# Windowed attention of a fused gate network: scores and values in 64x64 products over the visible keys only, values in two banks, and another order of steps

## The reference, cut to what matters

```python
WINDOW = 128
bk, bv = look_around(bk), look_around(bv)      # keys of the window before, then of this one: 256
sim = jnp.einsum('bhwid,bhwjd->bhwij', bq, bk) # 128 queries x 256 keys
mask = (i < j) | (i > j + WINDOW) | (j == -1)
sim = jnp.where(mask, -jnp.finfo(sim.dtype).max, sim)
attn = jax.nn.softmax(sim, axis=-1)
out = jnp.einsum('bhwij,bhwjd->bhwid', attn, bv)
```

## Time and profile before

| what | value |
|---|---|
| median of 3 runs | 5209.54 us (5208.2 to 5211.27) |
| the profiled execution | 5208.83 us |
| its span in the trace | 5207.0 us |
| granted TensorE clock over the span | 0.997 |
| PE matmul busy | 5089.8 us, 98% |
| DVE busy | 3371.8 us, 65% |
| ACT busy | 2933.1 us, 56% |
| POOL busy | 2614.3 us, 50% |

### The profile page before, as it was taken

The page is one execution under the profiler, slowest core; times in us unless marked ns, Lnnn a source line. Parts: engine busy times, 40 slices in busy tenths (PEclk is TensorE's granted clock), DMA queues, the critical chain, the costliest instruction groups (busy, mean ns, idle before and its releaser), DMA issues.

```text
span 5207.0 us, 177128 instructions
## 1 busy us (share of the span) xinstructions
PE 5089.8 (98%) x72856; PEld 4142.8 (80%) x72856; DVE 3371.8 (65%) x8313; ACT 2933.1 (56%) x7591; POOL 2614.3 (50%) x2308
## 2 busy tenths in 40 slices
PE   7999999999999999999999999999999999999998
PEld 5887888878888788887888887788777887878787
DVE  6656676666766667666676665766657676566764
ACT  4556555555555565555655556555556555565554
POOL 5445555455544456444464543645436455455543
PEclk9999999999999999999999999999999999999999
DMA  2211111111111211111121111201211112111110
GB/s 82 98 69 54 59 36 66 46 65 48 39 62 47 71 42 39 63 61 56 42 67 36 62 55 46 65 31 62 66 41 60 43 51 67 46 54 59 35 50 17
DMA packets 51392, 280.81 MB, mean 54 GB/s; under 512 B 5280, under 2 KB 22688, under 8 KB 33696
## 3 DMA queue, kind: packets, MB, share of 16 engines
q1 hardware_dynamic: 39840, 252.69, 13.2%
q0 software_dynamic: 10752, 16.78, 1.7%
HBM read 249.01 MB, written 28.84 MB: 53 GB/s over the span
## 4 chain that ended last, share of the span: by engine, by line
PE 96%; issue 1%; DVE 1%; ACT 1%; POOL 1%; SPq 0%; DMA 0%; POOLq 0%; ACTq 0%; DVEq 0%
PE bank_M L729 11%; PE bank_S L712 10%; PE bank_S L714 9%; PE bank_S L713 9%; PE bank_F L660 7%; PE bank_F L661 6%; PE bank_F L662 6%; PE bank_F L916 6%; PE bank_M L748 5%; PE bank_F L806 5%; PE bank_M L837 5%; PE bank_F L849 4%; PE bank_F L821 4%; PE bank_M L756 2%; PE bank_F L788 1%
## 5 line engine op out<-in xcount | busy, mean ns | idle before, releaser
L1497 POOL TENSOR_TENSOR q_lo<-q_mix,q_hi 128x512 fp32r<-128x512 f32 x512 | 668.4, 1306 | 1233.6 <-ACT q_hi L981 1233.6
L994 ACT ACTIVATE probs<-bank_S,neg_max 128x512 f32<-128x512 f32 x1024 | 700.9, 685 | 778.8 <-DVE neg_max L1227 688.7
L1227 DVE TENSOR_REDUCE neg_max<-bank_S 128x1 f32<-128x512 f32 x1024 | 696.2, 683 | 303.3 <-PE bank_S L714 300.0
L712 PE MATMUL bank_S<-k_hi,q_lo 128*128 128x512 f32 x2048 | 876.8, 428 | 7.2 <-POOL q_lo L1497 5.1
L714 PE MATMUL bank_S<-k_hi,q_hi 128*128 128x512 f32 x2048 | 805.7, 393 | 0.0
L713 PE MATMUL bank_S<-k_lo,q_hi 128*128 128x512 f32 x2048 | 805.0, 393 | 0.0
L729 PEld LDWEIGHTS bank_M<-mixer_n,probs 64*64 64x64 f32 x32768 | 528.1, 135 | 188.9 <-issue 165.8
L1492 POOL TENSOR_TENSOR q_mix<-q_rope,w_pre 128x256 f32<-128x256 f32 x1024 | 631.6, 638 | 52.2 <-POOL q_lo L1497 0.9
L1523 POOL TENSOR_TENSOR l_probs<-l_probs,l_inv 128x1024 f32<-128x1024 f32 (+1 forms) x256 | 429.2, 1682 | 396.1 <-DVE l_inv L1330 396.1
L729 PE MATMUL bank_M<-mixer_n,probs 64*64 64x64 f32 x32768 | 600.4, 222 | 14.0 <-issue 9.9
L1053 ACT ACTIVATE l_probs<-l_probs,l_least 128x256 f32<-128x256 f32 (+1 forms) x1024 | 480.5, 472 | 185.2 <-DVE l_least L1310 183.6
(11 more groups left out here) (142 smaller groups left out, 10173.8 us busy)
## 6 DMA issues: line engine op xcount, KB each, us to landing
w_qkv_hi<-split_qkv SPq DMA_DIRECT2D x30, 1536.0 KB, 6.7
w_qkv_lo<-split_qkv SPq DMA_DIRECT2D x30, 1536.0 KB, 6.3
w_hi<-split SPq DMA_DIRECT2D x30, 1408.0 KB, 6.1
w_lo<-split SPq DMA_DIRECT2D x30, 1408.0 KB, 8.3
w<-in_w SPq DMA_DIRECT2D x32, 768.0 KB, 4.2
w_o<-in_w_o SPq DMA_DIRECT2D x32, 512.0 KB, 5.2
x_in<-in_x POOLq DMA_DIRECT2D x16, 512.0 KB, 3.8
out_y<-in_x SPq DMA_DIRECT2D x16, 512.0 KB, 7.7
```

Source lines behind the costliest of these rows:

```text
L712: mm(bank[k][:], q_lo[q], k_hi[:, s, :], start=(s == 0), stop=False)
L994: fn(probs[:, n % PB, :], bank[k][:], ACT.Exp, bias=neg_max[:, n % 2:n % 2 + 1], accum_out=row_sum[:, n % 4:n % 4 + 1]).then_inc(emptied[k ...
L1227: v.tensor_reduce(neg_max[:, n % 2:n % 2 + 1], bank[k][:], AX.X, ALU.max, negate=True)\
L1497: g.tensor_tensor(q_lo[:, c % QB], q_mix[:], q_hi[:, c % QB].bitcast(F32), ALU.subtract)\
```

## The change

Scores: each product takes 64 queries (half a window) and only the keys that these may see, 192 for t > 0; for t = 0 it takes 64 keys for the lower queries and 128 for the upper ones. Head of the pair (row half of the PE array) and query half (column half) make four 64x64 tiles. Values: each product takes 64 keys, 64 features and 64 queries; keys 0-63 of a window go to bank M0, keys 64-127 to M1, and the two wholly masked blocks are left out (24 products instead of 8; 16 instead of 4 for t = 0). ACT copies M0 to `o_locT`, then DVE adds M1 to it in place of its copy. A `local_values` thus needs both M banks, which it holds until both are done.

```diff
+SEEN = P // 2
+BLOCKS_SEEN = [((0, 0, True, False), (0, 0, True, True)), ((0, 1, False, True), (1, 0, True, False)),
+               ((1, 1, True, True), (1, 1, False, True))]
+BLOCKS_AT_START = [((0, 1, True, True),) * 2, ((1, 1, True, True),) * 2]
...
     if kind == "local_values":
-        return [LOCAL]
+        return ["M0", "M1"]
...
                 for pair in range(2):
                     hp = 2 * quad + pair
-                    for parity in range(2):
-                        k = f"F{parity}"
-                        rows = slice(HD * parity, HD * (parity + 1))
-                        last = mm(bank[k][:, pair * 2 * P + lo:(pair + 1) * 2 * P],
-                                  qT[rows, hp, t * P:(t + 1) * P],
-                                  kT[rows, hp, (t - 1) * P + lo:(t + 1) * P], start=True, stop=True)
-                        if pair == 1:
-                            last.then_inc(filled[k], 1)
+                    for half in range(2):
+                        queries = slice(half * SEEN, (half + 1) * SEEN)
+                        first = P if t == 0 else half * SEEN
+                        final = P + (half + 1) * SEEN
+                        for parity in range(2):
+                            rows = slice(HD * parity, HD * (parity + 1))
+                            last = mm(bank[f"F{parity}"][queries, pair * 2 * P + first:pair * 2 * P + final],
+                                      qT[rows, hp, t * P + queries.start:t * P + queries.stop],
+                                      kT[rows, hp, (t - 1) * P + first:(t - 1) * P + final], start=True, stop=True)
+                            if pair and half:
+                                last.then_inc(filled[f"F{parity}"], 1)
...
-                if now.was_filled(step, LOCAL):
-                    pe.wait_ge(emptied[LOCAL], now.fill(step, LOCAL) - 1)
-                lo = 1 if t == 0 else 0
+                for k in banks_of(step):
+                    if now.was_filled(step, k):
+                        pe.wait_ge(emptied[k], now.fill(step, k) - 1)
                 for pair in range(2):
-                    for j in range(lo, 2):
-                        for parity in range(2):
-                            h = 4 * quad + 2 * pair + parity
-                            last = mm(bank[LOCAL][HD * parity:HD * (parity + 1), pair * P:(pair + 1) * P],
-                                      v_loc[:, t - 1 + j, h * HD:(h + 1) * HD], pT[:, pair, 2 * parity + j, :],
-                                      start=(j == lo), stop=(j == 1))
-                last.then_inc(filled[LOCAL], 1)
+                    for one in (BLOCKS_SEEN if t else BLOCKS_AT_START):
+                        for r, (half, j, start, stop) in enumerate(one):
+                            keys = slice(r * SEEN, (r + 1) * SEEN)
+                            for parity in range(2):
+                                h = 4 * quad + 2 * pair + parity
+                                last = mm(bank[f"M{r}"][HD * parity:HD * (parity + 1),
+                                                        pair * P + half * SEEN:pair * P + (half + 1) * SEEN],
+                                          v_loc[keys, t - 1 + j, h * HD:(h + 1) * HD],
+                                          pT[keys, pair, 2 * parity + j, half * SEEN:(half + 1) * SEEN],
+                                          start=start, stop=stop)
+                            if pair and one[0][0]:
+                                last.then_inc(filled[f"M{r}"], 1)
...
+            def local_values(step, l, u):
+                t, quad = u // QUADS, u % QUADS
+                act.wait_ge(filled["M0"], now.fill(step, "M0"))
...
+                fn(o_locT[:, 2 * quad:2 * quad + 2, :], bank["M0"][:, 0:2 * P].rearrange("p (c i) -> p c i", c=2), ACT.Copy)\
+                    .then_inc(emptied["M0"], 1)
...
-                dve.wait_ge(filled[LOCAL], now.fill(step, LOCAL))
...
-                v.tensor_copy(o_locT[:, 2 * quad:2 * quad + 2, :],
-                              bank[LOCAL][:, 0:2 * P].rearrange("p (c i) -> p c i", c=2)).then_inc(emptied[LOCAL], 1)
+                dve.wait_ge(filled["M1"], now.fill(step, "M1"))
+                dve.wait_ge(emptied["M0"], now.fill(step, "M0"))
+                to = o_locT[:, 2 * quad:2 * quad + 2, :]
+                v.tensor_tensor(to, bank["M1"][:, 0:2 * P].rearrange("p (c i) -> p c i", c=2), to, ALU.add)\
+                    .then_inc(emptied["M1"], 1)
```

All three order texts are replaced. Of `ORDER` two lines before and after show the kind of edit:

```diff
-up.1.1 scores.63 mixers.31 mix.30 norm up.1.2 up.1.3 mix.31 scale up.1.4 values.7 x_turn.0 talk_v up.1.5 talk_k talk_q
-down.1.0 down.1.1 down.1.2 down.1.3 project.3
+up.1.3 up.1.4 up.1.5 mix.30 x_turn.0 scores.62 scores.63 mixers.31 down.1.0 talk_q mix.31 talk_k values.7 down.1.1
+down.1.2 talk_v project.3 down.1.3
```

More of the change, by code:

```diff
@@ new lines @@
+scores.47 sigmoid.2 sigmoid.3 part.25 expand.26 mix.22 weigh.1.5 weigh.1.6 mixers.23 local_scores.1.7 out_proj.1.1
+scores.48 mix.23 part.26 scores.49 local_values.1.4 p_turn.1.5 mixers.24 scores.50 expand.27 part.27 expand.28
+values.5 scores.51 mix.24 mixers.25 scores.52 weigh.1.7 part.28 local_values.1.5 p_turn.1.6 scores.53 mix.25
+out_proj.1.2 mixers.26 local_values.1.6 p_turn.1.7 expand.29 scores.54 local_values.1.7 scores.55 mix.26 part.29
+out_proj.1.3 project.2 half_turn.1 mixers.27 expand.30 scores.56 shift_turn.1 mix.27 part.30 scores.57 scores.58
@@ L220 @@
[L220 to L223 removed]
+expand.0 part.0 expand.1 part.1 bound expand.2 qkv.0.0 join.0.0 scores.0 scores.1 qkv.0.1 part.2 q_turn.0.0 k_turn.0.0
@@ new lines @@
+out_proj.0.2 local_values.0.6 p_turn.0.7 mixers.10 part.13 scores.22 local_values.0.7 scores.23 out_proj.0.3 mix.10
+expand.14 half_turn.0 part.14 mixers.11 scores.24 shift_turn.0 mix.11 scores.25 values.2 h_scale.0 scores.26 mixers.12
+h_turn.0 scores.27 mix.12 scores.28 mixers.13 expand.15 up.0.0 up.0.1 mix.13 part.15 expand.16 up.0.2 up.0.3 up.0.4
+part.16 expand.17 up.0.5 part.17 scores.29 scores.30 expand.18 mixers.14 down.0.0 down.0.1 down.0.2 down.0.3 mix.14
+x_turn.1 scores.31 scores.32 mixers.15 qkv.1.0 join.1.0 part.18 expand.19 mix.15 qkv.1.1 join.1.1 q_turn.1.0 scores.33
@@ new lines @@
+local_values.1.6 mixers.26 p_turn.1.7 part.28 scores.54 local_values.1.7 scores.55 expand.29 mix.26 mixers.27 part.29
+out_proj.1.3 half_turn.1 mix.27 shift_turn.1 scores.56 expand.30 scores.57 project.2 mixers.28 values.6 h_scale.1
+part.30 expand.31 scores.58 mix.28 h_turn.1 scores.59 scores.60 mixers.29 up.1.0 part.31 up.1.1 up.1.2 up.1.3 up.1.4
+up.1.5 end.silu scores.61 mix.29 mixers.30 down.1.0 down.1.1 down.1.2 down.1.3 end.bound scores.62 scores.63 end.gated
+end.sigmoid.0 mixers.31 mix.30 end.sigmoid.1 mix.31 values.7 end.sigmoid.2 end.sigmoid.3 project.3 end.store
```

146 lines of the change are left out of this document (79 added, 67 removed).

## The result

The changed kernel took 5255.3 us (median of 4 runs, 5243.9 to 5259.2), the kernel before 5210.4 beside it. The ratio is 1.0082, with the interval 1.0065 to 1.0100: slower, by 45 us, where 77 fewer were forecast.

A forecast was written before the change was run, and what follows sets the result against it. PE, busy 98% of the span, was taken as the bound. 5208.8 - 66 (products, blocks and neighbours) - 33 (waits removed) + 22 (waits added) = 5132 us; the range ran from 5092 to 5175 us.

The forecast's parts named there:

- The products: On PE at t > 0, `local_scores` falls from 1.07 to 0.86 us, `local_values` from 1.02 to 0.85: 40 and 33 us saved.
- D: In `local_scores`, tiles with 192 columns run only two abreast: 121 us more, 5253 us, slower; chance 0.02.
- The blocks: In PE's step list, blocks of tiled steps rise from 737 to 893: 156 x 0.21 = 33 us lost.
- The neighbours of equal shape: On PE, adjacent 64x64 steps (`mix`, `local_scores`, `local_values`) each save 0.13 us, 209 times: 27 us gained.
- B: On PE, neighbours of equal tile shape pay for the change all the same: 5159 us; chance 0.18.
- What the new order removes: PE's idle time ahead of `talk_v` and `half_turn.0` goes, 24 and 8 us; -33 us booked in all.
- What it adds: New PE waits behind `local_values`, for banks and `o_locT` freed by ACT's copy then DVE's addition: +22 us, ends 8 to 45.
- The places that were walked: In `ORDER`: `local_values.0.7` 10 us; `out_proj.1.3` and `mix.23` together 6 us; `mix.9` and `mix.24` nothing to 0.1 us.
- For what I did not walk: Other places in `ORDER`, where ACT holds off its copy behind four exponentials: 0.4 us a batch, 6 us.
- Rival C: After `local_values`, the ACT-DVE chain sets PE's pace, up to 5353 us; chance 0.03 near a 0.39 us mean wait, 0.03 beyond.
- the break-even: Mean PE wait of 0.39 us after each of 256 `local_values`, 99 us in all, from which the change is slower.
- its full exposure: PE waits the whole 0.95 us ACT-DVE chain after each `local_values`: 243 us, giving 5353 us.

The follow-up runs named there:

- the kernel with LOCAL in M0: Kernel before with old products and old order but two steps, `local_values` in the one bank M0 instead of M1: 5366.0 us, ratio 1.0296.
- moving one word: Changed kernel with `store` moved in `ORDER` from just ahead of `mix.10` to behind `mixers.8`: 5228.0 us, ratio 1.0043.
- one third of the change, plus one word: Kernel before with only the 64x64 scores, old order, and `talk_v` moved behind `up.1.5`: 5147.7 us, ratio 0.9883.
- the scores alone in an order of its own: Kernel before with only the 64x64 scores, and some 90 of the 351 steps of the old `ORDER` moved: 5187.1 us, ratio 0.9959.

## Why the prediction was wrong

Point by point, by the prediction's steps:

- **The products.** Right. `local_scores` 0.81 us (0.86 forecast), `local_values` 0.86 (0.85). In two traces with the same list, old and new products, the `local_scores` steps sum to 37.5 us less from start to start and the `local_values` to 27.7 less, though some new waits stand in these sums. Tiles of 192 columns run four abreast; D is out.
- **The blocks.** Right in kind, too large in size: 0.13 us each against 0.21, +20 against +33, once the clock is taken out of the 28 us.
- **The neighbours of equal shape.** Right. A `mix` ahead of a `local_scores` takes 0.98 us and not 1.09, at 113 places, and a `local_values` of t > 0 ahead of one 0.72 and not 0.86. That is 0.11 and 0.14 where 0.13 was forecast; B is out. A `values`, whose tiles have another shape (128x32), takes its 1.92 us whether a `local_scores` follows or a step of full size. So the saving is there between steps of one tile shape and not between two shapes.
- **What the new order removes.** Right by the list of waits: 24 and 8 us.
- **What it adds: +22 us. This step failed.** Idle time rose by 92.5 us, on top of the 32 that went: about 124 were added. The places that were walked came out near: `local_values.0.7` 0.80 us, 11 us in all (10 forecast; the old products in the new order have the same wait, so it is the order's), `out_proj.1.3`, `mix.9` and `mix.24` 6 together. It was the line "For what I did not walk 0.4 us a batch, 6 us" that stood for nearly everything. It hid three errors.
  - I walked what stands behind a `local_values` and needs its banks. I did not walk what stands ahead of it and holds M0. That is 26.1 us in the new order, the waits for ACT's `mixed`. In the old one holding M0 costs 159 us, ahead of the step and behind it, shown by the kernel with LOCAL in M0.
  - I priced the new order by the two waits that it removes and by the blocks, and did not look for waits of its own at steps that the products do not touch: `store` behind its place (22.2 us, shown by moving one word), `k_turn` behind POOL (0.9 to 16.2 us), `mix.0` and `mix.6` 11 us from start to start. All of them stand in the run with the old products too. Nor did I see that faster scores shorten the cover over DVE's copy of M1 (9.0 us).
  - I booked nothing for PE's idle time without a releaser. It went from 27.4 to 52.1 us. The last section shows what ends it.
- **Rival C** named the mechanism's neighbourhood, with 0.03 beyond the break-even. In the old order the two banks cost 232/256 = 0.9 us a `local_values` net, near to its full exposure. In the new one the mean is well below its 0.39. Its argument against itself, that PE hardly waits for ACT or DVE before, was no evidence: M0, which ACT copies behind a `mix`, was then no bank of `local_values`. By the prediction's own sign, over 100 us of waits for `o_locT` or the M banks, C did not come: the list has 68 us of them, 22 of which end with the output's DMA.
- **Rival D** gives 5253 us, almost what was measured. That is chance: its `local_scores` above 1 us is not there.

So the gain from the products, some 65 us, is real and was spent twice: the order that makes room for two banks costs 39 us by itself, and within it the waits for M0 and M1 and the stalls without a releaser take what the products save. From 5246.5 to 5255.3 us, with intervals that overlap, the products in the new order are worth nothing.

## What to carry to other kernels

When an operation gets a second buffer, list that buffer's other users in both directions: who must have emptied it ahead of this operation, on which engine's queue, and behind what. An engine at 56% can hold a bank for 2 us, since its queue's order decides and not its load. And when a change comes in parts, time each part alone: the best kernel here was one third of the change, plus one word.

## What the hardware showed that was not expected

PE stands inside dense runs of small products with nothing to wait for. A `values` step of the changed kernel, split by such a stall, in the timeline of PE:

```profile
2922.61 1.77 PE L754 MATMUL bank_M<-mixed,v_heads 128*32 128x64 f32 x112
2925.95 0.43 PE L754 MATMUL bank_M<-mixed,v_heads 128*32 128x64 f32 x16 [1.57 <-issue]
```

The page names no releaser, but the trace of the DMA queues has one. Instructions come over a queue of their own, in packets of 16 KB that take about 1 us: 584 packets before (9.57 MB), 661 now (10.83 MB). The packet ahead of this stall ended at 2924.66, and PE went on 1.29 us later. It is so every time: all 53 waits of PE without a releaser in the changed kernel end 1.21 to 1.61 us after the end of such a packet, and so do all 32 of the kernel before (1.20 to 1.55 us). Of all matmuls of the changed kernel only 7% start 1.15 to 1.65 us after a packet's end. So in these stalls PE waits for its instructions. What would bring the packets earlier is open, since no kernel changed the supply alone.

Summed over all stalls over 0.1 us inside steps, in us:

| | old order | new order |
|---|---|---|
| old products | 25.6 | 15.8 |
| the same, `local_values`' products halved | not run | 21.0 |
| 64x64 scores alone | 31.7 | 30.4 |
| values in two banks alone | 26.2 | not run |
| both | 31.3 | 49.2 |

The number of instructions doesn't decide alone: both kernels of the last row have the same, and the stalls are fewer where PE waits for banks for longer. Nor does the pace: the scores alone in an order of its own have 39.0 us, at 5187 us.

A second surprise is the price of an instruction count by itself: the same 128 columns as two products of 64 cost a `local_values` 57 ns for 16 more matmul instructions, each with its weight load.
